# Attention weights kept as low and high halves, contiguous per block of keys, with one 512-column matmul for both

## The reference

```python
xn = _layernorm(x, axis=-1)
qkv = jnp.einsum('bsd,ed->bse', x, Wqkv).reshape(B, S, 3 * H, D)     # H = 16, D = 128
q, k, v = qkv[:, :, :H], qkv[:, :, H:2 * H], qkv[:, :, 2 * H:]
logits = jnp.einsum('bqhd,bkhd->bhqk', q, k) * D ** (-0.5)
w = jax.nn.softmax(logits.astype(jnp.float32), axis=-1)
out = jnp.einsum('bhqk,bkhd->bqhd', w, v).reshape(B, S, H * D)
return jnp.einsum('bse,de->bsd', out, Wout)
...
x = x + attention(xn, Wqkv, Wout) + ffn(xn, w1, w2, w3)
```

## Time and profile before

| what | value |
| --- | --- |
| median of three runs | 1956.21 us (1951.72 to 1957.82) |
| profiled execution | 1959.55 us, its span 1957.7 us |
| granted TensorE clock | 0.994 of full speed |
| busy: PE, DVE, POOL, ACT | 97%, 82%, 69%, 64% of the span |
| DMAs that move weights (L257) | 2048 of 128 KB, 2.4 us from issue to landing |

### The profile page before, as it was taken

One profiled execution on the slowest core, in us unless ns is written; L12 is line 12 of the kernel. 1 busy time (PEld: TensorE's weight loads), 2 busy tenths in 40 slices (PEclk: granted clock), 3 DMA queues, 4 the chain that ended last, 5 costly groups with the idle time before them and its releaser, 6 DMA issues.

```text
span 1957.7 us, 33299 instructions
## 1 busy us (share of the span) xinstructions
PE 1894.0 (97%) x11556; PEld 1694.3 (87%) x11556; DVE 1599.0 (82%) x2088; ACT 1251.4 (64%) x1698; POOL 1355.2 (69%) x514
## 2 busy tenths in 40 slices
PE   5979999999999999999999999999999999999997
PEld 4859898998888899888888989888998889889886
DVE  6378888888888888888888888788888888888883
ACT  3446676666666676666667666666766667666663
POOL 2417676776767677676767777676776767687676
PEclk9999999999999999999999999999999999999998
DMA  3046667676767767676776767677676767767675
GB/s 104 1 104 153 161 162 175 151 177 157 165 144 166 175 149 175 159 165 143 169 175 148 174 159 168 142 170 175 148 177 159 163 156 165 177 146 175 146 166 136
DMA packets 197241, 302.45 MB, mean 154 GB/s; under 512 B 38144, under 2 KB 57280, under 8 KB 197056
## 3 DMA queue, kind: packets, MB, share of 16 engines
q1 hardware_dynamic: 197056, 300.11, 65.6%
HBM read 12.65 MB, written 2.10 MB: 8 GB/s over the span
## 4 chain that ended last, share of the span: by engine, by line
PE 59%; POOL 13%; issue 11%; SPq 9%; DVE 3%; ACT 2%; DMA 2%; POOLq 0%; DVEq 0%; ACTq 0%
POOL pt L975 11%; SPq L257 8%; PE ps_o L354 8%; PE ps_o L356 8%; PE ps_o L355 8%; PE ps_s L342 7%; PE ps_s L344 7%; PE ps_s L343 7%; PE ps_t L332 3%; PE ps_s L313 3%; PE ps_t L322 3%; DMA pt<-prob 2%; PE ps_s L388 2%; DVE prob L840 1%; POOL v_lo L966 1%
## 5 line engine op out<-in xcount | busy, mean ns | idle before, releaser
L975 POOL TENSOR_TENSOR pt<-pt,pt_hi 128x2048 fp32r<-128x2048 f32 x256 | 1181.4, 4615 | 477.6 <-ACT pt_hi L621 476.3
L629 ACT ACTIVATE prob<-ps_s,neg_max 128x1024 f32<-128x1024 f32 x512 | 566.9, 1114 | 467.0 <-DVE neg_max L831 466.9
L840 DVE STREAM_TRANSPOSE prob<-prob 128x1024 f32<-128x1024 f32 x512 | 612.8, 1232 | 162.9 <-ACT prob L629 162.9
L827 DVE TENSOR_REDUCE row_max<-ps_s 128x1 f32<-128x1024 f32 x512 | 619.8, 1215 | 65.7 <-PE ps_s L344 36.3
L354 PE MATMUL ps_o<-pt_hi,v_hi 128*128 128x256 f32 x2048 | 583.8, 285 | 13.5 <-POOL v_lo L966 6.8
L356 PE MATMUL ps_o<-pt_hi,v_lo 128*128 128x256 f32 x2048 | 582.6, 284 | 0.0
L355 PE MATMUL ps_o<-pt,v_hi 128*128 128x256 f32 x2048 | 580.6, 284 | 0.0
L621 ACT CAST pt_hi<-pt 128x2048 fp32r<-128x2048 f32 x256 | 491.1, 1919 | 137.5 <-DMA pt<-prob 130.9
L342 PE MATMUL ps_s<-k_hi,q_hi 128*128 128x512 f32 x1024 | 403.9, 394 | 22.8 <-ACT prob L629 17.3
L354 PEld LDWEIGHTS ps_o<-pt_hi,v_hi 128*128 128x128 f32 x2048 | 388.1, 189 | 22.5 <-POOL pt L975 7.2
L344 PE MATMUL ps_s<-k_hi,q_lo 128*128 128x512 f32 x1024 | 401.1, 392 | 0.0
(11 more groups left out here) (95 smaller groups left out, 1667.8 us busy)
## 6 DMA issues: line engine op xcount, KB each, us to landing
pt<-prob SPq DMA_DIRECT2D x2048, 128.0 KB, 2.4
v_raw<-v_turned SPq DMA_DIRECT2D x244, 64.0 KB, 2.0
w_raw<-wqkv_dram SPq DMA_DIRECT2D x32, 128.0 KB, 2.5
y<-x_dram SPq DMA_DIRECT2D x4, 512.0 KB, 5.6
wo_raw<-wqkv_dram SPq DMA_DIRECT2D x16, 128.0 KB, 2.5
wo_raw<-wo_dram SPq DMA_DIRECT2D x16, 128.0 KB, 2.2
out_dram<-y SPq DMA_DIRECT2D x8, 256.0 KB, 2.9
w_raw<-w_dram SPq DMA_DIRECT2D x2, 704.0 KB, 8.8
```

Of the source, the lines that this page charges most:

```text
L629: nc.scalar.activation(prob[:, t % E_RING, half * HALF:(half + 1) * HALF], ps_s[:, 2 * half:2 * half + 2, :].rearrange("p b n -> p (b n)") ...
L827: nc.vector.reduce_max(row_max[:, t, half:half + 1], ps_s[:, 2 * half:2 * half + 2, :].rearrange("p b n -> p (b n)"), AX_X).then_inc(s_mx, 1)
L840: nc.vector.transpose(tile, tile).then_inc(s_xp, 1)
L975: nc.gpsimd.tensor_tensor(raw, raw.bitcast(F32), pt_hi.rearrange("p t (i x) -> p (t i) x", i=4)[:, :, col], ALU.subtract).then_inc(s_pl, 1)
```

## The change

The raw weights that the DMAs bring now go to `raw`, a ring of two pairs. ACT and POOL write the high and the low part from there into a third buffer, `parts`, in which the low and the high columns of a key block lie side by side: 512 contiguous columns per block of keys. The product of a key block is then two matmuls: the high values against all 512 columns, whose result is 256 columns "high values by low weights" and 256 columns "high values by high weights", and the low values against the 256 high columns. The two halves of the result are no longer added in PSUM: `output_low` has a second instruction on DVE that adds them.

```diff
-RAW_RING = 3
+RAW_RING = 2
...
-        pt = sb("pt", [P, RAW_RING, 2, S], F32R)
-        pt_hi = sb("pt_hi", [P, 2, S], F32R)
+        raw = sb("raw", [P, RAW_RING, 2, S])
+        parts = sb("parts", [P, T, 2, 8, BLK], F32R)
...
+        def moved(p, half):
+            return raw[:, p % RAW_RING].rearrange("p t (i b q) -> p (t i) b q", i=4, q=BLK)[
+                :, :, half * KH:(half + 1) * KH, :]
+        def half_of(which, half):
+            return parts[:, half * KH:(half + 1) * KH, which].rearrange("p b a q -> p a b q")
...
                 for p in range(PAIRS):
                     sp.wait_ge(s_xp, count(32, h, 4 * p + 4))
+                    if h[0] or p >= RAW_RING:
+                        sp.wait_ge(s_pl, count(16, h, 2 * (p - RAW_RING) + 2))
...
-                    nc.tensor.matmul(dst, v_hi[:, kb, :], hi[:, :, col], start=(kb == 0), stop=False)
-                    nc.tensor.matmul(dst, v_hi[:, kb, :], lo[:, :, col], start=False, stop=False)
-                    last = nc.tensor.matmul(dst, v_lo[:, kb, :], hi[:, :, col], start=False, stop=(kb == T - 1))
+                    nc.tensor.matmul(ps_pv, v_hi[:, kb, :], parts[:, kb].rearrange("p s a q -> p (s a q)"),
+                                     start=(kb == 0), stop=False, skip_group_check=True)
+                    last = nc.tensor.matmul(ps_pv_hi, v_lo[:, kb, :], parts[:, kb, 1].rearrange("p a q -> p (a q)"),
+                                            start=False, stop=(kb == T - 1), skip_group_check=True)
...
-                nc.scalar.copy(pt_hi.rearrange("p t (i x) -> p (t i) x", i=4)[:, :, col],
-                               pt[:, slot(h, p)].rearrange("p t (i x) -> p (t i) x", i=4)[:, :, col].bitcast(F32)
+                nc.scalar.copy(half_of(1, half), moved(p, half)).then_inc(s_ph, 1)
...
-                if t % 2 and half and reused:
-                    dve.wait_ge(s_pv, count(16, h, 2 * (t // 2 - RAW_RING) + 2))
...
-                nc.vector.tensor_tensor(o_lo[:], ps_pv, o_hi[:], ALU.subtract).then_inc(s_olo, 1)
+                nc.vector.tensor_tensor(o_lo[:], ps_pv_hi, o_hi[:], ALU.subtract).then_inc(s_orest, 1)
+                dve.wait_ge(s_orest, count(8, h, p + 1))
+                nc.vector.tensor_tensor(o_lo[:], ps_pv_lo, o_lo[:].bitcast(F32), ALU.add).then_inc(s_olo, 1)
...
+                nc.gpsimd.tensor_tensor(half_of(0, half), moved(p, half), half_of(1, half), ALU.subtract
+                                        ).then_inc(s_pl, 1)
...
-            with pe.Fori(1, H - 5, RAW_RING) as it:
-                for n in range(RAW_RING):
-                    head((it, n, (n + 1) % RAW_RING), False, False)
-            for n in (3, 2, 1):
-                head((H - n, 0, (H - n) % RAW_RING), False, n == 1)
+            with pe.Fori(1, H - 2) as it:
+                head((it, 0), False, False)
+            for n in (2, 1):
+                head((H - n, 0), False, n == 1)
```

More of the change, by code:

```diff
@@ L293, in _ @@
             move_values(3, v_turned, s_vmv)
-            head((0, 0, 0), 9)
-            with sp.Fori(1, H - 5, RAW_RING) as it:
-                for n in range(RAW_RING):
-                    head((it, n, (n + 1) % RAW_RING), 9)
-            for n in (3, 2, 1):
-                head((H - n, 0, (H - n) % RAW_RING), n - 1)
+            for n in range(H):
+                head((n, 0), H - 1 - n)
             out_v = out_d.rearrange("(t p) c -> p t c", p=P)
@@ L446, in product_step @@
                     pe.wait_ge(s_vlo, count(2, h, half + 1))
-                products(h, p, half)
+                products(half)
             def output_step(h, p):
@@ L514, in head @@
                         keys(bank)
-            head((0, 0, 0), True, False)
-            with pe.Fori(1, H - 5, RAW_RING) as it:
-                for n in range(RAW_RING):
-                    head((it, n, (n + 1) % RAW_RING), False, False)
-            for n in (3, 2, 1):
-                head((H - n, 0, (H - n) % RAW_RING), False, n == 1)
-            end = (H - 1, 0, (H - 1) % RAW_RING)
+            head((0, 0), True, False)
+            with pe.Fori(1, H - 2) as it:
+                head((it, 0), False, False)
+            for n in (2, 1):
+                head((H - n, 0), False, n == 1)
+            end = (H - 1, 0)
             product_step(end, 5, 1)
@@ L576, in _ @@
             for part in (1, 0, 2):
-                part_high(part, (0, 0, 0), 0)
+                part_high(part, (0, 0), 0)
             for b in range(FB + 1):
@@ L684, in head @@
                         keys_high(after(h), bank)
-            head((0, 0, 0), True, False)
-            with act.Fori(1, H - 5, RAW_RING) as it:
-                for n in range(RAW_RING):
-                    head((it, n, (n + 1) % RAW_RING), False, False)
-            for n in (3, 2, 1):
-                head((H - n, 0, (H - n) % RAW_RING), False, n == 1)
-            end = (H - 1, 0, (H - 1) % RAW_RING)
+            head((0, 0), True, False)
+            with act.Fori(1, H - 2) as it:
+                head((it, 0), False, False)
+            for n in (2, 1):
+                head((H - n, 0), False, n == 1)
+            end = (H - 1, 0)
             output_high(end, 5)
@@ L915, in head @@
                         keys_low(after(h), bank)
-            head((0, 0, 0), True, False)
-            with dve.Fori(1, H - 5, RAW_RING) as it:
-                for n in range(RAW_RING):
-                    head((it, n, (n + 1) % RAW_RING), False, False)
-            for n in (3, 2, 1):
-                head((H - n, 0, (H - n) % RAW_RING), False, n == 1)
-            end = (H - 1, 0, (H - 1) % RAW_RING)
+            head((0, 0), True, False)
+            with dve.Fori(1, H - 2) as it:
+                head((it, 0), False, False)
+            for n in (2, 1):
+                head((H - n, 0), False, n == 1)
+            end = (H - 1, 0)
             result(end, 4, 1)
@@ L954, in _ @@
             for part in (1, 0, 2):
[L955 removed]
+                part_low(part, (0, 0), 0)
             with pool.Fori(0, G) as g:
@@ L1009, in head @@
                         values_low(h, 1)
-            head((0, 0, 0), True, 9)
-            with pool.Fori(1, H - 5, RAW_RING) as it:
-                for n in range(RAW_RING):
-                    head((it, n, (n + 1) % RAW_RING), False, 9)
-            for n in (3, 2, 1):
-                head((H - n, 0, (H - n) % RAW_RING), False, n - 1)
-            end = (H - 1, 0, (H - 1) % RAW_RING)
+            head((0, 0), True, 9)
+            with pool.Fori(1, H - 2) as it:
+                head((it, 0), False, 9)
+            for n in (2, 1):
+                head((H - n, 0), False, n - 1)
+            end = (H - 1, 0)
             denominator(end, 7)
```

39 lines of the change are left out of this document (14 added, 25 removed).

## The result

| | kernel before | kernel after |
|---|---|---|
| median of the runs, us | 1954.81 (1951.72 to 1957.82) | 1928.13 (1927.06 to 1929.79) |
| profiled execution, us | 1959.55 | 1928.06 |
| span, us | 1957.7 | 1926.2 |

What follows compares the result with a forecast made beforehand. PE's matmuls were taken to bound the middle heads. Terms -25 - 9.2 + 12.6 + 1.3 = -20.3 us took the profiled 1959.55 to 1939.3, and 3.3 us less for the median gave 1936 us, range 1917 to 1958.

Steps and rivals of the forecast that it cites:

- The matmuls, -25 us: Key block on PE from 0.360 to 0.347 us, taken as 0.012 gained over 2048 blocks: -25 us.
- what goes is one start of a matmul per block, and no more: PE's product keeps the same 768 columns per key block, so merging saves only one matmul start, taken as 0.012 us.
- Its bound of -16: Smaller end of the matmul gain, with 512-column matmuls up to 0.232 us apart and 0.008 us gained per block.
- The jumps, -9.2 us: Loop jumps back: three stalls of 3.9 us go (-11.6), 12 short-body seams cost +2.4, together -9.2 us.
- the 0.2 us put on each of the 12 new seams: Allowance for each jump back of the changed kernel's one-head loop: +2.4 us in all.
- Given back in the heads, +12.6 us: SP's new wait and PE's wait for low values cost 0.9 us per head in 14 heads: +12.6 us.
- So 0.44 us arrives at the logits of tile 11: SP's pair 2 moves wait 0.44 us longer for POOL's pair 0 subtraction, delaying DMAs, ACT's exponentials and those logits.
- PE's longer wait for the low values: At a head's first product PE comes about 0.45 us earlier and waits so much longer than its 0.43 us.
- nothing is given back: Rival: the two waits hide in each other, leaving -33 us and 1923 us; chance 0.15.
- DVE's second instruction: Added instruction in output_low, about 0.43 us, 8 per head, covered by PE's 0.77 us; bounds 0 to 1.8 us per head.
- POOL's and ACT's writes in runs: Writing runs of 32 elements costs 0, between ends of 0 and 2.4 us per subtraction; POOL's stays at 4.6 us.
- The end, +1.3 us: Behind the last tile three outputs follow each other with PE waiting, 3 x 0.43 us: +1.3 us.

Runs made afterwards that it cites:

- before_flat: Kernel before with no loop over heads, all five engines' heads written out: 1942.31 us, ratio 0.9932.
- strided3: three_matmuls with the parts laid out as before the change, so a matmul reads 8 runs of 32 columns: 1938.73 us, ratio 0.9908.
- three_matmuls: Changed kernel with three 256-column matmuls per key block, all into the same PSUM columns, and one instruction in output_low: 1910.99 us, ratio 0.9786.
- three_split: three_matmuls with the high-by-low product sent to the other half of the PSUM bank and added by DVE: 1915.96 us, ratio 0.9793.
- pe_body3: Changed kernel with PE's loop alone written over three heads, other engines at one head per trip: 1929.29 us, ratio 0.9876.
- grouped: Changed kernel with all eight 512-column matmuls of a half product first, then its eight 256-column ones: 1916.39 us, ratio 0.9811.
- x_operand: Changed kernel with the wide product's 512 moving columns taken from the transposed x, leaving out part of the computation: 1916.74 us, ratio 0.9805.
- x_both: Changed kernel with both weights and 512 moving columns of the wide product taken from the transposed x: 1917.88 us, ratio 0.9811.

## Why the prediction came out as it did

Put in a row, each step with one change against the one above, the ratios give this account of the 26.7 us:

| step | ratio | us |
|---|---|---|
| kernel before | 1 | |
| its jumps gone (before_flat) | 0.9932 | -13.3 |
| ring of two, one buffer for the parts (strided3) | 0.9908 | -4.7 |
| parts contiguous per block (three_matmuls) | 0.9786 | -23.9 |
| two sums, DVE adds them (three_split) | 0.9793 | +1.4 |
| one wide matmul for two (changed kernel) | 0.9864 | +13.9 |

Each ratio is uncertain by 0.0015, 3 us. So the step of 1.4 may be nothing, and that of 4.7 is hardly clear of it; the latter changes several things at once (the buffers, SP's wait, short bodies for no loops) and was not taken apart. Its heads 1 to 14 are even (3.4 us less in all than in before_flat), which pe_body3 suggests to be PE's fetching gone; that is argued, not tested. The profiles agree in sign and roughly in size: by their heads, over 15 of them, contiguity is worth (112.45 - 110.5) x 15 = 29 us and the wide matmul costs (111.54 - 110.55) x 15 = 15. The last step holds for wide and narrow matmuls in turn, as the change has them; grouped gets most of it back.

- **The matmuls, -25 us: mis-sized, and for a reason that was wrong.** The step that failed is "what goes is one start of a matmul per block, and no more". A wide matmul takes 0.227 where PE is at its best (the logits and the projection of three_matmuls, 1.36 / 6) and a narrow one 0.113 to 0.114 (its half product of 2.74 / 24), half of it: there is no start to save. By the heads this term is -14 us ((112.45 - 111.54) x 15), by the ratios -9 (the last three steps). It is the sum of a gain that the prediction did not see, the contiguous operand (-24 by the ratios, -29 by the heads), and of a loss by the merging (+14 and +15). In the earlier trace rows 256 columns took 0.120 and 512 took 0.227; I read the surplus of 0.0065 over half of 0.227 as a start. The greater part of it was the access pattern: the logits' operand is one run, the product's was 8. The rest stays with contiguous operands too, 0.118 behind logits, and why is open.
- **Its bound of -16**, from the 0.232 of L332, was just missed: blocks of 0.353 give 0.007 x 2048 = -14.
- **The jumps, -9.2 us: right in kind, a little small.** Bodies of one head pass their jump without a stall, on DVE, ACT and PE alike, as POOL's did; bodies of three heads bring it back. The jumps of before were worth 13.3, within the noise of the 11.6 of the prediction, and the 0.2 us put on each of the 12 new seams is zero: heads are even to 0.02 us. SP's hole went with its loop. The earlier trace rows could not have shown a stall of POOL: the records have its jump at 552.51, ahead of the subtraction of 553.13, and that subtraction would have covered 3 us. The records of the jump itself bear the premise out. POOL's next instruction there stands 0.2 us behind it. With bodies of three heads DVE's stand 3.0 to 3.5 us behind and ACT's 3.1 to 3.5; with one head 0.3 and 0.2. From branch to branch the records count 193 instructions on DVE, 163 on ACT and about 60 on POOL for one head, and these pass; 573 on DVE, 477 on ACT and 510 on SP for three heads stall, 173 on POOL do not. PE has 1139 matmuls and loads in a head, and over 3400 in three. PE's jump takes its queue 3.3 to 3.9 us with three heads and 0.2 with one; in pe_body3 the matmuls queued ahead cover it. The prediction divided only the counted instructions, without waits and jumps (130 and 106 for one head), and chose rightly all the same.

- **Given back in the heads, +12.6 us: wrong.** The steps "So 0.44 us arrives at the logits of tile 11" and PE's longer wait for the low values both failed, and the fault lies in the rows chosen. The earlier trace rows are of head 8, and that head took 113.2 us. In head 9 of the same trace of the kernel before, which took 112.4, POOL shows

```profile
1169.70 2.45 POOL L966 TENSOR_TENSOR v_lo<-v_raw,v_hi 128x1024 fp32r<-128x1024 f32 x1
1172.08 4.64 POOL L975 TENSOR_TENSOR pt<-pt,pt_hi 128x2048 fp32r<-128x2048 f32 x1
```

and DVE the turned blocks of pair 2:

```profile
1175.23 2.43 DVE L840 STREAM_TRANSPOSE prob<-prob 128x1024 f32<-128x1024 f32 x2 [0.28 <-ACT prob L629]
```

  POOL ends at 1176.72, the blocks at 1177.66: 0.94 us of room instead of -0.44. The low values are there at 1172.15, and PE's product starts at 1172.99. So both chains had room in an undisturbed head, and I priced them by a disturbed one, times 14. Some of that room was used up, as the prediction said: in the changed kernel 0.58 us is left of 0.94, and 0.56 of 0.84 in front of the product. PE's 0 us of loss in head 9 had said so, and stood as an argument for the rival "nothing is given back", which got 0.15.
- **DVE's second instruction: right.** Its cost was put at nothing. three_split against three_matmuls is the test of this, together with the second sum: 1.4 us, with an uncertainty that is larger. 425 ns were forecast as 430.
- **POOL's and ACT's writes in runs: right**, 4631 ns against 4615.
- **The end, +1.3 us:** not seen; from the first logits of the last head to the end it is 140.6 us, before it was 140.5.

The total of -20.3 is close to the -26.7 by luck: the matmuls gained 11 us less than forecast by the heads and 16 less by the ratios, nothing of the 12.6 was given back, and these two nearly cancel. The 6 us between the totals are what is left, with the jumps and the step of 4.7, which the prediction had not.

## What to carry to other kernels

Before merging matmuls to save starts, divide the pitch by the columns for every shape and access pattern that the trace shows: here 256 columns cost at best half of 512, and the money lay in a contiguous moving operand. Make one change at a time of layout and of shape; the change as made hid a loss of 14 us behind a gain of 24, and the kernel with three narrow matmuls on contiguous parts (1911 us) is the better one. A loop body of up to 193 instructions (on PE, one head) cost nothing at its jump. Bodies of three heads cost 1.9 us a jump on DVE and 2.4 to 3.1 on four engines, and on PE alone next to nothing at the jump but some 3 us spread over the heads. The size of the body, not the number of jumps, decided. And a wait is to be priced in a head that runs undisturbed, not in the one in which it shows best.

## What the runs showed of the hardware

- PE's pace in a run of like matmuls is not one number: 256 contiguous columns come at 0.113 to 0.114 us or at 0.118 (both in three_matmuls, by the place in the program) and at 0.113, then 0.119 to 0.120 in the output projection of every kernel; 8 runs of 32 come at 0.116 to 0.124 once the run has settled. At a granted clock of 1.00 in all stretches shown it is no matter of the clock.
- PE's pace also depends on the matmuls ahead. The six wide ones of a projection behind a half product take 1.387 us in the changed kernel and 1.388 before, and 1.360 in three_matmuls, x_operand and x_both. This does not follow the time of the half product ahead, which is 2.82 in the changed kernel and 2.83 in three_matmuls.
- Fetching of PE's code is followed by slow DMA issues on SP. Of its some 2110 issues in the heads that wait for nothing, 77 took over 700 ns in the kernel before (101 fetch packets), 12 in the changed one (20 packets), 58 with PE's body of three heads (82) and 67 in before_flat (90). Between the changed kernel and pe_body3 only PE's loop differs, so PE's body brings them; how it does is open.
- Code comes in packets of 8 KB on q14, one for 128 instructions of SP, and of 16 KB on PE's q8, one for 256 on average (before_flat).
